# Graph attention and mixture of experts on one core: node rows gathered per chunk into a ring, not per step

## The reference, cut to what matters

```python
# x: 6250 x 256; src, dst: 100000 edges, sorted by dst; 8 heads of 32
xn = layernorm(x)
h = einsum('ni,hio->hno', xn, W)
attn_src, attn_dst = (h * a_src).sum(-1), (h * a_dst).sum(-1)      # head x node
z = leaky_relu(attn_src[:, src] + attn_dst[:, dst], 0.2)
p = exp(z - z.max())
s = segment_sum(p.T, dst, 6250)
out = segment_sum((p / (s[dst].T + 1e-10))[..., None] * h[:, src], dst, 6250)
x1 = x + out + xn
# then a layernorm, a top-2-of-16 mixture of experts (256 -> 512 -> 256),
# another layernorm with gamma and beta, and a second residual
```

## Time and profile before

| | |
|---|---|
| median of 3 runs | 1836.19 us (1834.32 to 1840.44) |
| the profiled execution | 1835.8 us, of which the span of the profile is 1834.0 us |
| edge stage | first gather starts at 96.6 us, last at 1165.7 us |
| busy share of the span | PE 75%, DVE 64%, ACT 41%, POOL 67% |
| mean granted TensorE clock | 0.825 |

### The profile page before, as it was taken

The page is one execution under the profiler, slowest core; times in us unless marked ns, Lnnn a source line. Parts: engine busy times, 40 slices in busy tenths (PEclk is TensorE's granted clock), DMA queues, the critical chain, the costliest instruction groups (busy, mean ns, idle before and its releaser), DMA issues.

```text
span 1834.0 us, 28107 instructions
## 1 busy us (share of the span) xinstructions
PE 1377.4 (75%) x6723; PEld 1059.1 (58%) x6723; DVE 1176.5 (64%) x3565; ACT 752.1 (41%) x2240; POOL 1231.3 (67%) x1237
## 2 busy tenths in 40 slices
PE   4936767677777767777776667657589999999965
PEld 3724444454444444444444444456479999999953
DVE  6757777777777777777776777699634443332346
ACT  2634444445454445444444444344323322332335
POOL 1267777777777777777777777327347767656746
PEclk9958888878887778777778888855589999999987
DMA  8344444444444444444444444236768778877874
GB/s 229 122 142 130 128 135 130 135 128 136 130 135 130 135 128 136 130 132 131 133 130 126 134 129 137 58 134 188 185 197 224 211 206 220 213 198 205 213 188 161
DMA packets 167985, 283.82 MB, mean 155 GB/s; under 512 B 33294, under 2 KB 94822, under 8 KB 167670
## 3 DMA queue, kind: packets, MB, share of 16 engines
q0 software_dynamic: 62256, 143.99, 31.5%
q1 hardware_dynamic: 102466, 137.18, 24.1%
q10 hardware_dynamic: 3108, 0.85, 0.3%
HBM read 240.57 MB, written 42.16 MB: 154 GB/s over the span
## 4 chain that ended last, share of the span: by engine, by line
PE 45%; POOL 24%; issue 10%; DMA 10%; DVE 9%; ACT 1%; DVEq 1%; ACTq 0%; POOLq 0%; SPq 0%
POOL region L767 23%; PE bank L911 12%; PE bank L1044 11%; PE bank L1056 11%; DMA region<-node_rows,region 8%; PE bank L846 2%; PE bank L1033 1%; PE bank L899 1%; PE bank L929 1%; PE bank L1081 1%; PE bank L936 1%; PE bank L963 1%; DVE z L1317 1%; DVE z L1312 1%; POOL region L833 1%
## 5 line engine op out<-in xcount | busy, mean ns | idle before, releaser
L767 POOL DMA_INDIRECT region<-node_rows,region x832 | 816.9, 982 | 287.0 <-issue 216.9
L911 PE MATMUL bank<-region 128*128 128x264 f32 x1664 | 602.9, 510 | 0.4 <-DVE region L1350 0.3
L1352 DVE TENSOR_TENSOR region<-region,bank 128x264 f32 x728 | 310.8, 427 | 225.1 <-PE bank L911 210.0
L911 PEld LDWEIGHTS bank<-region 128*128 128x128 f32 x1664 | 379.8, 246 | 69.5 <-DVE region L1338 0.7
L1338 DVE TENSOR_TENSOR region<-region 128x512 f32<-128x512 f32 x416 | 284.6, 685 | 3.1 <-ACT region L639 3.1
L625 ACT ACTIVATE region<-iota_row,region 128x128 f32<-128x128 f32 x832 | 262.5, 386 | 0.0
L635 ACT ACTIVATE neg_max<-bank 128x1 f32<-128x1 f32 x104 | 17.8, 171 | 584.2 <-PE bank L936 584.2
L699 ACT ACTIVATE region<-bank,b_col 128x128 f32<-128x128 f32 x452 | 129.2, 368 | 310.3 <-PE bank L1044 310.2
L929 PE MATMUL bank<-ident,zmax 128*1 128x128 f32 x104 | 34.5, 332 | 294.6 <-DVE zmax L1323 294.6
L827 POOL DMA_INDIRECT sum_rows<-region,row_u x113 | 179.6, 1589 | 110.8 <-DVE region L1703 49.0
L1044 PEld LDWEIGHTS bank<-region 128*128 128x128 f32 x1808 | 220.8, 193 | 5.7
(11 more groups left out here) (239 smaller groups left out, 1525.1 us busy)
## 6 DMA issues: line engine op xcount, KB each, us to landing
region<-in_L_ffn_w SPq DMA_DIRECT2D x129, 512.0 KB, 8.7
region<-dloc_rows SPq DMA_DIRECT2D x104, 256.0 KB, 3.5
region<-node_rows,region POOLq DMA_INDIRECT x832
node_rows<-region SPq DMA_DIRECT2D x12, 528.0 KB, 3.1
y_rows<-region SPq DMA_DIRECT2D x7, 896.0 KB, 4.7
sum_rows<-region SPq DMA_DIRECT2D x7, 896.0 KB, 7.1
region<-in_x SPq DMA_DIRECT2D x6, 896.0 KB, 10.5
region<-sum_rows SPq DMA_DIRECT2D x5, 896.0 KB, 11.2
```

The lines of the kernel that those rows point to most:

```text
L767: p.indirect_dma_start(gathered[g % SLOTS][:, j, :], None, node_rows, bass.IndirectOffsetOnAxis(src_idx[:, k:k + 1], 0)).then_inc(row_in[g ...
L911: pe.matmul(bank[AGG_BANKS[k % AGG]][:, 0:ROW], onehot[:, (g % 3) * GROUP + j, :], gathered[g % SLOTS][:, j, :], start=True, stop=True).th ...
L1352: v.tensor_tensor(rows, rows, new, ALU.add).then_inc(acc_add)
```

## The change

The ring holds 32 chunks (`RING`), one row buffer of 272 words each, and POOL gathers each of the 782 chunks once; a chunk that serves several steps stays in its place. A chunk's place may be overwritten when the last step of the chunk 32 before it is aggregated. Which place a step reads is a number that the chip computes in the first stage, packed into `slot_row`; DVE, ACT and PE each load 8 such numbers per group (`slots_of`), POOL loads 8 counts per 16 chunks (`first_steps_of`), and ACT loads 8 more per group, the counts at which the rows have landed (`landings_of`).

A node row is now 8 heads of 34 words: attn_src, 32 of h, and a 1. Since the places of a group are no longer side by side, ACT copies attn_src out of 8 places into `asrc` (`attention_of_rows`), after the one-hots of the group before; DVE's add reads `asrc` and waits for it. p goes to a buffer of its own. Before it is used, `one_outside` adds 1 to p where the edge belongs to another tile, so that multiplying leaves those rows as they were for a later step on the same chunk. `weigh` takes one step per instruction, 33 of 34 words of each head (h and the 1, so the sums come out with the rows), and waits for the `weigh` before it.

The first stage loses the padded copy of src and 7 of 14 small indirect fetches and gains 7 transposes and some small table operations; `landings` is five more DVE operations ahead of the groups.

```diff
-ROW = F_IN + HEADS
+WIDE = F_OUT + 1
+ROW = HEADS * WIDE
+NODE_WIDE = WIDE + 1
+NODE = HEADS * NODE_WIDE
+RING, LANDS = 32, 8
...
-            for g in range(GROUPS):
...
-                for j in range(GROUP):
-                    k = g * GROUP + j
-                    if g >= SLOTS and j % 2 == 0:
-                        p.wait_ge(agg_mm, (g - SLOTS) * GROUP + j + 2)
-                    p.indirect_dma_start(gathered[g % SLOTS][:, j, :], None, node_rows,
-                                         bass.IndirectOffsetOnAxis(src_idx[:, k:k + 1], 0)).then_inc(row_in[g % SLOTS], 16)
+            for c in range(CHUNKS):
...
+                if c >= RING and c % 2 == 0:
+                    n = (c - RING) // 2
+                    if n % GROUP == 0:
+                        counts = first_steps_of(n)
+                    p.wait_ge(agg_mm, c - RING + 2)
+                    p.wait_ge(agg_mm, counts[n % GROUP])
+                p.indirect_dma_start(place(c), None, node_rows, bass.IndirectOffsetOnAxis(src_idx[:, c:c + 1], 0)
+                                     ).then_inc(row_in[c * LANDS // RING % LANDS], 16)
...
+            def attention_of_rows(g):
+                words = slots_of(s, g)
+                if g >= 2:
+                    s.wait_ge(z_add, g - 1)
...
+                    counts = landings_of(s, g)
+                    s.wait_ge(p_ok, g - 1)
+                    for i in range(LANDS):
+                        s.wait_ge(row_in[i], counts[i])
+                for j in range(GROUP):
+                    ins = copy(asrc[:, g % 2, j, :], rows_at_slot(words[j])[:, :, 0])
+                ins.then_inc(asrc_ok)
...
                 onehots(g)
+                if g + 1 < GROUPS:
+                    attention_of_rows(g + 1)
...
             def edge_logits_add(g):
                 zg = z[:, g % 2, :, :]
                 v.wait_ge(z_sum, g + 1)
-                v.wait_ge(row_in[g % SLOTS], GROUP * landed(g, SLOTS))
-                v.tensor_tensor(zg, zg, gathered[g % SLOTS][:, :, F_IN:ROW], ALU.add).then_inc(z_add)
+                v.wait_ge(asrc_ok, g + 1)
+                v.tensor_tensor(zg, zg, asrc[:, g % 2, :, :], ALU.add).then_inc(z_add)
...
-            def weigh(g, quarter):
+            def one_outside(g):
                 v.wait_ge(p_ok, g + 1)
-                js = slice(quarter * 2, quarter * 2 + 2)
-                hv = gathered[g % SLOTS][:, js, 0:F_IN].rearrange("p j (h o) -> p j h o", o=F_OUT)
-                pv = gathered[g % SLOTS][:, js, F_IN:ROW].unsqueeze(3).broadcast_to([P, 2, HEADS, F_OUT])
-                v.tensor_tensor(hv, hv, pv, ALU.mult).then_inc(weigh_ok)
+                v.scalar_tensor_tensor(p_buf[:, g % 2, :, :], z[:, g % 2, :, :], -FAR / 16, p_buf[:, g % 2, :, :],
+                                       ALU.is_lt, ALU.add).then_inc(outside_ok)
+
+            def weigh(g, j, word):
+                k = g * GROUP + j
+                if j == 0:
+                    v.wait_ge(outside_ok, g + 1)
+                if k >= 1:
+                    v.wait_ge(weigh_ok, k)
+                hv = rows_at_slot(word)[:, :, 1:NODE_WIDE]
+                v.tensor_tensor(hv, hv, p_buf[:, g % 2, j, :].unsqueeze(2).broadcast_to([P, HEADS, WIDE]),
+                                ALU.mult).then_inc(weigh_ok)
```

More of the change, by code:

```diff
@@ L340, in landed, with x_gathered @@
             return 16 * (i // ring + 1)
+        def x_gathered(j):
+            return 16 * sum(c * LANDS // RING % LANDS == j % XG for c in range(CHUNKS)) + landed(j, XG)
         def y_landed(q):
@@ L360, in junk_of, with place, rows_at_slot @@
             return junk[:, start:start + width]
[L363 to L367, removed]
+        def place(c):
+            n = (c + RING_FIRST) % RING * NODE
+            return ring[:, n:n + NODE]
+        def rows_at_slot(word):
+            return by_head(ring[:, bass.ds(word, NODE)], NODE_WIDE)
+        FIRST_DYNAMIC_G = RING // GROUP - 1
         Z_BANKS, M_BANK, AGG_BANKS = (2, 3), 4, (0, 1, 5, 6, 7)
@@ L421, in tiles_of, with slots_of, landings_of, first_steps_of @@
             return tiles
+        def slots_of(eng, g):
+            _, words = nc.values_load_multi_w_load_instructions(
+                slot_row[0:1, g * GROUP:(g + 1) * GROUP], engines=[eng.engine], min_val=0, max_val=(RING - 1) * NODE,
+                skip_runtime_bounds_check_because="a slot's number, which is below the ring's, times its words")
+            return words
+        def landings_of(eng, g):
+            _, counts = nc.values_load_multi_w_load_instructions(
+                land[0:1, g, :], engines=[eng.engine], min_val=16, max_val=16 * CHUNKS,
+                skip_runtime_bounds_check_because="16 for each gather, from the ring's first ones on, by construction")
+            return counts
+        def first_steps_of(n):
+            _, counts = nc.values_load_multi_w_load_instructions(
+                first_row[0:1, n:min(n + GROUP, FIRSTS)], engines=[mybir.EngineType.Pool], min_val=2, max_val=STEPS,
+                skip_runtime_bounds_check_because="a chunk's first step is at least its own number")
+            return counts
         def scatter_waits_of(back, j):
@@ L901, in attn_dst_of, with aggregate @@
                 ins.then_inc(ad_mm)
-            def aggregate(g, js):
+            def aggregate(g, js, words):
                 for j in js:
@@ L930, in tensor_program @@
                 if last:
-                    aggregate(g - 2, range(1, 4))
+                    aggregate(g - 2, range(1, 4), words)
                 if now:
@@ L938, in tensor_program @@
                 if last:
-                    aggregate(g - 2, range(4, 6))
+                    aggregate(g - 2, range(4, 6), words)
                 if more:
@@ L947, in tensor_program @@
                 if last:
-                    aggregate(g - 2, range(6, GROUP))
+                    aggregate(g - 2, range(6, GROUP), words)
                 if g == GROUPS:
@@ L1380, in vector_program @@
             late_groups()
+            landings()
             for g in range(GROUPS + 2):
@@ L1400, in vector_program @@
                         onehots_t(g + 1)
+                    if now and j == 3:
+                        one_outside(g)
                     if now and j >= 4:
-                        weigh(g, j - 4)
+                        weigh(g, 2 * (j - 4), words[2 * (j - 4)])
+                        weigh(g, 2 * (j - 4) + 1, words[2 * (j - 4) + 1])
                     if g == GROUPS and j < 3:
```

205 lines of the change are left out of this document (149 added, 56 removed).

## The result

The changed kernel takes 2037.32 us (median of 4 runs, 2036.25 to 2041.04) against 1837.39 us: a ratio of 1.110 (95% interval 1.108 to 1.111). The profiled execution took 2036.44 us, with a span of 2034.6 us against 1834.0.

What follows compares the result with a forecast made beforehand. POOL was taken to bound the kernel before at 10.31 us a group, DVE the changed one at 11.86: 103 x (11.86 - 10.31) = +160, and +2 for first and last stage, on 1835.8 gives 1998 us; own range 1940 to 2045.

Steps and rivals of the forecast that it cites:

- The bound before, POOL, and its 64 us: POOL's gathers set the pace of the kernel before; 50 fewer at 1.287 us each free 64 us.
- DVE's list: DVE's own sequence of instructions per group takes 11.86 us in the changed kernel and sets the pace.
- The circle through ACT: Per group, DVE's add to ACT's L635, one-hots, loads, eight copies and back to the next add: 10.96 us.
- Two multiplies where one was: 1.34 us from add to add: On DVE, the second multiply waits for the first; add-to-add spacing goes from 0.95 to 1.34 us, four times a group.
- Loads in the open: about 0.8 us idle ahead of the sum: DVE's two register loads, 0.596 us each, follow a waiting multiply and leave the sum idle 0.8 us before it.
- The add of step 4 at 5.2: `one_outside` holds DVE's add of step 4 back to about 5.2 us into the group, from 5.11.
- the rival of the cold TensorE: PE's clock stays low in a group's second half: 13.2 us a group, 2136 us; chance 9%.
- First and last stage: 2 us: Outside the groups, `landings` and the first copies add 2 us, of 0 to 6.
- POOL's loads at nothing: POOL's 47 added loads of 8 counts, at most 94 us, were taken as 0, off the path.
- POOL stays the bound: Rival: added copies and multiplies fit in ACT's and DVE's idle time, giving 1774 us; chance 8%.
- register loads are slow: Rival: DVE's register loads cost POOL's 2.0 us each, 14.67 us a group, 2287 us; chance 2%.
- Waits of DVE for itself are free: Rival: 0.29 us comes off each of four multiply pairs, the path through ACT decides at 10.96, 1905 us; chance 12%.

Runs made afterwards that it cites:

- e8: The kernel before with 50 gathers left out and nothing else changed, so its output is not the reference's: 1778.93 us, ratio 0.969.
- e1: The changed kernel with DVE's two register loads per group moved from ahead of the sum to behind the add of step 0: 1925.97 us, ratio 1.047.
- e2: The changed kernel with one multiply behind each of DVE's eight adds, instead of two behind each of four: 1900.72 us, ratio 1.032.
- e7: The kernel before with each multiply over two steps split into two over one step, the second waiting for the first: 1860.23 us, ratio 1.012.
- e3: The changed kernel with seven more copies per group on ACT ahead of its eight, to a place nothing reads: 2037.98 us, ratio 1.108.
- e4: The changed kernel with ACT's loads and copies for the next group moved between the two halves of its one-hots: 2037.87 us, ratio 1.108.
- e5: The changed kernel with DVE's loads behind the add of step 0 and one multiply behind each add: 1901.64 us, ratio 1.035.

## Why the prediction was right, point by point

- **The bound before, POOL, and its 64 us.** Right, and shown by e8, 58 us.
- **DVE's list is the longer path.** Shown by e1, e2 and e7 on one side, e3 and e4 on the other. The circle through ACT stood close behind, as forecast: in e5 it is the limit.
- **Two multiplies where one was: 1.34 us from add to add.** Measured 1.27; the second starts 0.57 after the first, not 0.64. The 0.21 of idle had been read between adds, which also read PE's bank; between multiplies it is 0.14.
- **Loads in the open: about 0.8 us idle ahead of the sum.** Measured 0.93. Each load takes 0.596 as priced, and the first starts with the last multiply (620.39 and 620.37), as assumed; from there to the sum it is 1.36 us, not 1.19. The reading of the kernel before was off: its load starts ahead of the last multiply (see e7), not with it.
- **The add of step 4 at 5.2.** This is the term that was too small, and in the trace it goes with the clock. It stood at 5.83 in the group shown and waited 0.46 us for an aggregate there. The path to the negated maximum was 0.2 longer than in the earlier trace rows (three aggregates at the lower clock take 3.00 us, not 2.91; why is open), and the two aggregates behind it took 1.91 us, against 1.16 at the same place one group earlier. That other group, and two windows of the one shown (busy times, then the granted clock ahead of the DMA share):

```profile
602.32 1.16 PE L1014 MATMUL bank<-region 128*128 x4
...
612.00:613.00 1.00, 1.00 (x4) 0.79 (x3) 0.74 (x3) 0.00 (x0) 0.00 (x0) 0.50 0.45 122
616.90:617.90 1.00, 1.00 (x4) 0.65 (x4) 0.86 (x4) 1.00 (x5) 0.69 (x2) 1.00 0.81 212
```

The granted clock is at 1.2 GHz in the first half of the group and back at 2.4 in the second, as in the earlier trace rows; but the return can fall behind aggregates 4 and 5. Sorted by the clock granted during those two, 33 of the 88 groups had 2.4 GHz throughout, and their add of step 4 comes at 5.20 on average, just as priced. 39 had 1.2 GHz throughout, and there it comes at 5.82; in the other 16 the clock changed meanwhile. In the kernel before it was 61, 14 and 13. So a part of the rival of the cold TensorE came true. That rival's reason, the longer period, is not shown: e7, at 10.56 us a group, has the low clock there in 57 of 88 groups. The prediction had argued against it from two aggregates that took 1.60 us; with 1.16 and 1.91 us for the two levels, 1.60 is a clock that came back only halfway through them (the trace has 0.50 in the first half, 0.92 in the second).

  The averages account for the 12.19 - 11.86 = 0.33 us a group: 0.32 from the add of step 4, 0.10 from there being 2.28 us between the last add and the sum, not 2.18, and 0.07 less for the three spacings between adds. The groups at 2.4 GHz still take 12.11 us, those at 1.2 GHz 12.38: the former wait 0.24 us later on, for the aggregate of step 6. No run changed the clock alone, so what it is worth in time stays an argument from groups of one execution.
- **The circle through ACT: 10.96 us.** The eight copies were bounded by 0.14 and 0.28 and priced at 0.20 apart: 1.6 us. They take 0.96: each lasts 0.20 but starts 0.11 after the start of the one before. The idle time ahead of them is 0.85, not 0.38. The second load ends 0.40 after the last one-hot (619.37 and 618.97), as priced; the rest is the string of waits for landed rows, a term that was left out. The page puts this idle time down to the gathers, which was named as a sign of being wrong, but none of the 400 recorded waits lasts over 0.04 us, so the rows had landed. Together 1.8 against 2.0; two errors cancel, and the group of e5 at 10.89 us agrees with the circle as priced. (Its upper bound adds up to 12.3, not 12.4.)
- **First and last stage: 2 us.** Measured 7.4 (4.9 ahead of the first group, 2.5 behind the last). The first gather starts 2.7 us later.
- **POOL's loads at nothing.** They take 0.565 us each, 47 of them, 27 us against 543.8 us of idle time.
- **Rivals.** "POOL stays the bound" fell with the result, and "register loads are slow" with the 596 ns. "Waits of DVE for itself are free" fell too: e7, with fixed addresses, spaces two multiplies 0.46 us apart (0.88 less 0.42), and with register addresses it is 0.57, where operations without such a wait start 0.34 apart. The Trainium skill ("VectorE: DVE Perf Modes", section "The DRAIN you can't avoid") measured no cost of a semaphore after each of a run of copies. These traces do not agree for the multiplies here.

The sum was 39 us short of 2037: 103 x 0.33 = 34 on the groups and 5 outside them. The mechanism was right. That 2037 lies inside the forecast's own range, near its top of 2045, owes something to errors that partly cancel: the multiplies were priced too dear, the clock's part too cheap.

## What to carry to other kernels

Before relieving the engine that bounds a loop, count what the relief adds to the engines behind it, in spacing and not in busy time: here 58 us could be had, and the price was four instructions per group that wait for their neighbour and two register loads of 0.6 us that had nothing to hide under, one of them new. Put an instruction that waits for its predecessor behind another that does not, and a register load where the engine waits anyway, but not ahead of what others wait for. And try a move again after the limit has changed: ACT's earlier copies were worth 0 us in the changed kernel and 62 us once DVE's list was short.

## What the runs showed of the hardware that was not expected

- In these runs a register load behind a multiply that waits on a semaphore started with that multiply (620.39 and 620.37 in the changed kernel, 601.19 and 601.18 in e7) and was in the open. Behind a multiply that need not wait it started 0.58 us ahead of it, and its 0.596 us were hidden. Splitting a multiply of the kernel before uncovered 0.30 us of a load that nobody had moved (e7).
- In a loop of 10 to 12 us the granted clock came back before or after the same two aggregates, group by group, and the add behind them came 5.20 or 5.82 us into the group. At a period of 10.3 us it was low for both of them in 14 of 88 groups (kernel before), at 10.56 in 57 (e7), at 12.19 in 39 (changed kernel): the share does not follow the period.
- Copies of 8 columns on ACT from SBUF last 0.20 us each and overlap: eight take 0.96 together.
- One chip ran the same kernel before 12% slower (2062 us against 1836), with waits of up to 2.5 us on POOL that the trace ends with "remote". On it a version that is 1.8% faster elsewhere showed a ratio of 1.002.
